# One transfer for each copy of x, and fp32 products in layer 0 of a recommender tower

## The chip, the cores and the metric

The kernel runs on one core of a Trainium2 chip. The metric is the device time of one execution in microseconds (us), the median of some runs. The core has five engines with instruction streams of their own, which meet only through semaphores: PE (TensorE, matrix products), DVE (VectorE), ACT (ScalarE), POOL (GpSimd) and SP, which issues most of the DMA transfers. Sixteen DMA engines carry the transfers of all queues.

## The reference

A compressed interaction network over looked-up embeddings, then a small dense tower. 1024 rows of the batch, 32 fields, 16 embedding columns, three layers of 128 outputs:

```python
e = jnp.stack([tbl_0[ids[:, 0]], ..., tbl_31[ids[:, 31]]], axis=1)     # 1024 x 32 x 16
x0 = h = e
for i in range(3):
    z = (x0[:, :, None, :] * h[:, None, :, :]).reshape(B, F * G, E)
    y = relu(einsum('oc,bce->boe', W[i], z) + b[i][None, :, None])
    x_keep, h = (y[:, :64], y[:, 64:]) if i < 2 else (y, y)
    xs.append(x_keep)
z = sum(concatenate(xs, axis=1), axis=2)                               # 1024 x 256
h = maximum(concatenate([z, dense_ctx], axis=1) @ W_top1 + b_top1, 0)
h = maximum(h @ W_top2 + b_top2, 0)
return h @ W_top3
```

Everything is float32. Layer 0 has 32 x 32 products of fields with themselves (symmetric, so that half of them suffice), layers 1 and 2 have 32 x 64 each.

## The kernel before

**Tiles.** A block is 128 rows of the batch, a tile is four embedding columns of a block: 512 columns (`COLS`) with 48 rows (`XROWS`, the 32 fields and the first 16 again). There are 32 tiles. On the partitions lie pairs of a field and a second index, 128 at a time; such a set is a chunk, two chunks are an item, and an item is one DVE product of 128 x 1024. Layer 0 has two items, (0, 0) and (0, 1), and a tail of one chunk, layers 1 and 2 have eight items each, (1, 0) to (2, 7).

**Copies of x.** To multiply x by itself shifted, and by h, x must lie on the partitions in several copies. ACT copies the transposed x into `xrows` (48 x 512), SP stores it in DRAM as `xcols` (line 383), waits until that has landed, and loads it back: `shifted` in four transfers, one for each group of 32 partitions (line 390), `shifted_tail` in four (line 395), and `spread` in groups of four chunks, two transfers for each group, one per half of 64 partitions, each of which repeats a row of x on 64 partitions (line 406). `spread` has two buffers, for even and odd tiles, and a group is loaded again once DVE has made the last product that reads it (the wait on `s_made` in `load_spread`).

**Order.** `SLOT` writes out the order of the items; all engines follow it. Slot s does layer 1 of tile s, layer 2 of tile s - 1 and layer 0 of tile s + 1, interleaved. SP does for each tile, in `load_factors`: `load_shifted` of the tile, the last group of `spread` for the tile before it, then groups 0 to 2 of its own. SP works strictly in that order, so a wait holds up all that stands behind it. The middle of the program is a hardware loop over blocks.

**Precision.** PE multiplies plain fp32 items (`WHOLE`, line 604), as layer 1 is done. The others are split: ACT rounds the product to fp32r (`high`, line 808), DVE or POOL subtracts to get the rest (`low`, lines 1051 and 490), and PE makes three passes with weights split the same way: high by high, high by low (line 612) and low by high (line 627). `kind_of` says which item is of which kind: layer 1 whole, layer 0 and item (2, 6) split by DVE, the rest of layer 2 by POOL; in the last slot other items of layer 2 go to DVE. Each kind has a ring of buffers, `RING = (4, 4, 2)`. POOL also does the lookups (line 480).

**Before the loop** the weights are transposed by PE and put in place by DVE, from a layout of layer 0 (`w0_dist`) in which chunk after chunk holds the field distances. `rotated` prepares the first tile's `shifted` without DRAM.

Of the kernel before, what the change touches and what calls it, by code (L numbers as in the profile page):

```python
# [33 lines left out]
F32 = mybir.dt.float32  # L34
# [4 lines left out]
P = 128  # L39
FIELDS = 32  # L40
# [44 lines left out]
RING = (4, 4, 2)  # L85
SPLIT2_BY_DVE = [(2, 6)]
LAST_BY_DVE = [(2, 2), (2, 5), (2, 7)]
# [74 lines left out]
def dlrm_tower(nc, dense_ctx, ids, tables, w_top1, b_top1, w_top2, b_top2, w_top3,  # L162
               w0, b0, w1, b1, w2, b2, xcols, out):
    batch = ids.shape[0]
# [6 lines left out]
    with ExitStack() as ctx:  # L171
# [21 lines left out]

        w0T_high = sb("w0T_high", [P, GROUP, P], F32R)
        w0T_low = sb("w0T_low", [P, GROUP, P], F32R)
# [3 lines left out]
        w2T_low = sb("w2T_low", [P, CHUNKS, P], F32R)  # L199
        wt3 = sb("wt3", [P, TOP2 // P])  # L200

# [165 lines left out]
        def _(sp):  # L367
# [11 lines left out]
            def load_shifted(t):  # L379


                sp.wait_ge(s_xrows, number(t) + 1)
                sp.dma_start(xcols[number(t)], xrows[:, :]).then_inc(s_xcols, 16)
                sp.wait_ge(s_xcols, 16 * (number(t) + 1))
                x = xcols[number(t)]
                if isinstance(t[0], int) and number(t) == 0:

                    return
                for j in range(GROUP):
                    sp.dma_start(shifted[FIELDS * j:FIELDS * (j + 1), :, :],  # L390
                                 bass.AP(x.tensor, x.offset + j * COLS,
                                         [[COLS, FIELDS], [GROUP * COLS, GROUP], [1, COLS]])
                                 ).then_inc(s_shifted, 16)
                for j in range(GROUP):
                    sp.dma_start(shifted_tail[FIELDS * j:FIELDS * (j + 1), :],
                                 x[FIELDS // 2:XROWS, :]).then_inc(s_shifted_tail, 16)

            def load_spread(t, g):
                x = xcols[number(t)]
# [42 lines left out]

            sp.wait_ge(s_made[BY_DVE], plan.entry((BLOCKS - 1, TILES_PER_BLOCK - 2), LAST0) + 1)
            sp.dma_start(wt1[:, :].rearrange("p (c n) -> p c n", n=TOP1),
# [95 lines left out]
        def _(pe):  # L540
# [8 lines left out]
            pe.wait_ge(s_ident, 1)  # L549
            pe.wait_ge(s_sym, 7)  # L550
            turn(0, GROUP, P, lambda c: w0_dist[:, P * c:P * (c + 1)])
# [17 lines left out]
            def turn_x(t):  # L569

                pe.wait_ge(s_four, number(t) + 1)
                if not (isinstance(t[0], int) and number(t) == 0):

                    pe.wait_ge(s_xrows, number(t))
                    pe.wait_ge(s_made[BY_DVE], plan.entry(after(t, -2), LAST0) + 1)
# [17 lines left out]
            def multiply(s, item):  # L593
# [6 lines left out]
                if kind == WHOLE:  # L600
                    z = prod[plan.place(s, item, RING)]
                    pe.wait_ge(s_made[kind], e + 1)
                    for c in range(ITEM):
                        last = pe.matmul(y[:, :], w1T[:, ITEM * n + c, :], z[:, c, :], start=(n == 0 and c == 0),  # L604
                                         stop=(item == LAST1 and c == ITEM - 1))
                    last.then_inc(s_used[kind], 1)
                else:
                    z = high[kind][plan.place(s, item, RING)]
                    pe.wait_ge(s_high[kind], e + 1)
                    for c in range(ITEM):  # L610
                        for w in ((w0T_high, w0T_low) if layer == 0 else (w2T_high, w2T_low)):
                            pe.matmul(y[:, :], w[:, ITEM * n + c, :], z[:, c, :],  # L612
                                      start=(n == 0 and c == 0 and w in (w0T_high, w2T_high)), stop=False)

            def multiply_low(s, item):
# [10 lines left out]
                for c in range(ITEM):  # L626
                    last = pe.matmul(accumulator(s, layer)[:, :], (w0T_high if layer == 0 else w2T_high)[:, ITEM * n + c, :],  # L627
                                     z[:, c, :], start=False, stop=(item in (LAST0, LAST2) and c == ITEM - 1))
                last.then_inc(s_used[kind], 1)
# [124 lines left out]
        def _(act):  # L754
# [29 lines left out]
            def take_x(t):  # L784
                act.wait_ge(s_xT, number(t) + 1)

                act.wait_ge(s_xcols, 16 * number(t))
                act.copy(xrows[:, :], xT[0:XROWS, :]).then_inc(s_xrows, 1)
# [21 lines left out]
            def next_h0(s):  # L810

                act.wait_ge(s_used[BY_DVE], plan.entry(s, LAST0) + 1)
                go_on(h0[(s[1] + 1) % 2], y0, 1, bias0, s_h0)
# [48 lines left out]
            def top_high(part):  # L862
# [10 lines left out]
                elif part == 3:  # L873
                    act.wait_ge(s_wt2, 16)

                    act.wait_ge(s_xT, TILES)
                    act.wait_ge(s_xcols, 16 * TILES)
                    copy = act.copy(wt2_high[:, :], wt2[:, :])
# [41 lines left out]
        def _(dve):  # L920
# [19 lines left out]
            dve.tensor_copy(w0_dist[:, FIELDS:FIELDS * H].rearrange("p (d f) -> p d f", f=FIELDS),  # L940
                            bass.AP(w0_wide.tensor, w0_wide.offset + 1,
                                    [list(w0_wide.ap[0]), [1, H - 1], [2 * FIELDS + 1, FIELDS]])).then_inc(s_sym, 1)
            dve.tensor_copy(w0_dist[:, 0:FIELDS], diagonal(w0_raw, FIELDS, 0, FIELDS)).then_inc(s_sym, 1)
# [4 lines left out]

            dve.wait_ge(s_sym, 6)
# [3 lines left out]
            homes = [w0T_high[:, :, :], w0T_tail[:, :]]  # L953
            homes += [w1T[:, GROUP * g:GROUP * (g + 1), :] for g in range(GROUPS)]
            homes += [w2T_high[:, GROUP * g:GROUP * (g + 1), :] for g in range(GROUPS)]
            lows = {0: w0T_low[:, :, :]}
            lows.update({2 + GROUPS + g: w2T_low[:, GROUP * g:GROUP * (g + 1), :] for g in range(GROUPS)})
            for n, home in enumerate(homes):
                dve.wait_ge(s_turned, n + 1)
                source = prep[1][:, 0, :] if n == 1 else prep[n % 2]  # L960
                if n == 1:
# [7 lines left out]
                    last.then_inc(s_stored, 1)  # L969
                elif n in lows:  # L970
                    dve.tensor_copy(home, source).then_inc(s_w_high, 1)

# [30 lines left out]
            for c in FIRST_ORDER:  # L1003
                dve.tensor_copy(rotated[c].rearrange("p (e a f) -> p e a f", a=GROUP, f=FIELDS),
                                bass.AP(unwrapped.tensor, unwrapped.offset + GROUP * c,
                                        [list(unwrapped.ap[0]), [XROWS, QUAD], [1 if c < GROUP else 0, GROUP], [1, FIELDS]])
                                ).then_inc(s_rotated, 1)

            def multiply(s, item):
# [6 lines left out]
                elif item == (0, 0):  # L1016
                    dve.wait_ge(s_shifted, 16 * GROUP * number(t))
                if item == (0, 0):
                    dve.wait_ge(s_xT, number(t) + 1)
                if item == TAIL:  # L1020
                    if not isinstance(t[0], int) or number(t) > 0:
                        dve.wait_ge(s_shifted_tail, 16 * GROUP * number(t))

# [177 lines left out]
```

## Time and profile before

| | us |
|---|---|
| median of 3 runs | 1115.0 |
| lowest and highest run | 1112.32 and 1119.09 |
| span of the profiled execution | 1109.1 |
| busy PE / DVE / POOL / ACT in it | 994.0 / 987.2 / 882.4 / 572.7 |

The span is the time from the first to the last instruction of the profiled execution; the runs also hold what lies around it. An engine's busy time leaves out its waits and its semaphore instructions. PE's busy time counts pipelined matmuls, whose ends are modelled, so starts that follow one another say more of its pace. Mean times in the groups come with a count, and "idle before" tells how long the engine stood just before such instructions and who released it.

### The profile page before, as it was taken

The numbers are of one execution on the slowest core, as the hardware profiler recorded it, in microseconds if no ns is written. First come the engines' busy times: TensorE is split into PE (matmuls) and PEld (weight loads), VectorE is DVE, ScalarE is ACT, GpSimd is POOL, SyncE is SP. The second block draws the span as 40 slices with busy tenths as digits, with TensorE's granted clock in tenths as the row PEclk, the third lists the DMA queues.
The fourth block names the chain that finished last, engine by engine and source line by source line (L and its number), as shares of the span: only waits on it lengthen the run. The fifth ranks groups of instructions, "written<-read, shape, count | busy, mean of one in ns | idle before, by whom it ended". The sixth has DMA issues, their size and how long they took to land.

```text
span 1109.1 us, 12343 instructions
## 1 busy us (share of the span) xinstructions
PE 994.0 (90%) x3281; PEld 611.0 (55%) x3281; DVE 987.2 (89%) x842; ACT 572.7 (52%) x683; POOL 882.4 (80%) x525
## 2 busy tenths in 40 slices
PE   3167989998997979999899989999899999999988
PEld 2134556564654646555556656555556656565665
DVE  6246999999996999999999999999999999999982
ACT  0234556554654545565555645565455556555553
POOL 7645899997977979997999979997999966665760
PEclk9588999998998999999899999999899999999999
DMA  6199989899886869898888879888788989888500
GB/s 118 14 195 198 184 170 190 195 186 191 168 192 133 164 163 199 175 194 177 168 183 182 195 174 193 184 186 190 156 182 179 192 194 191 185 197 193 124 1 1
DMA packets 111813, 184.55 MB, mean 166 GB/s; under 512 B 19570, under 2 KB 24178, under 8 KB 111540
## 3 DMA queue, kind: packets, MB, share of 16 engines
q1 hardware_dynamic: 103604, 182.24, 76.8%
q0 software_dynamic: 8192, 2.11, 1.9%
q8 instruction: 8, 0.13, 0.1%
q14 instruction: 9, 0.07, 0.0%
HBM read 181.15 MB, written 3.15 MB: 166 GB/s over the span
## 4 chain that ended last, share of the span: by engine, by line
POOL 29%; DVE 18%; issue 18%; DMA 15%; PE 13%; ACT 4%; SPq 2%; DVEq 1%; POOLq 0%; ACTq 0%
POOL low L490 15%; POOL looked_up L480 12%; DVE unsplit L1043 9%; DMA xcols<-xrows 6%; PE y L604 6%; DMA shifted<-xcols 5%; DVE prod L1043 4%; PE y L612 4%; PE y L627 2%; POOL tail_parts L498 2%; DMA spread<-xcols 1%; SPq L390 1%; DMA looked_up<-in_tbl,ids_now 1%; ACT h L794 1%; DVE tail L1025 1%
## 5 line engine op out<-in xcount | busy, mean ns | idle before, releaser
L490 POOL TENSOR_TENSOR low<-unsplit,high 128x1024 fp32r<-128x1024 f32 x222 | 543.7, 2454 | 110.5 <-ACT high L808 108.3
L808 ACT CAST high<-unsplit 128x1024 fp32r<-128x1024 f32 x320 | 334.0, 1047 | 330.2 <-DVE unsplit L1043 322.7
L604 PE MATMUL y<-prod,w1T 128*128 128x512 f32 x1024 | 491.4, 609 | 5.1 <-ACT kept L800 2.7
L480 POOL DMA_INDIRECT looked_up<-in_tbl,ids_now x256 | 291.3, 1138 | 69.3 <-issue 58.6
L1043 DVE TENSOR_TENSOR prod<-spread,h 128x1024 f32<-128x1024 f32 x256 | 307.1, 1210 | 7.9 <-ACT h L794 7.4
L1043 DVE TENSOR_TENSOR unsplit<-spread,h 128x1024 f32<-128x1024 f32 x256 | 307.7, 1212 | 4.2 <-ACT h L794 4.2
L604 PEld LDWEIGHTS y<-prod,w1T 128*128 128x128 f32 x1024 | 196.0, 195 | 171.1 <-issue 149.5
L627 PE MATMUL y<-low,w2T_high 128*128 128x512 f32 x512 | 222.5, 518 | 48.4 <-POOL low L490 47.5
L612 PE MATMUL y<-high,w2T_high 128*128 128x512 f32 x512 | 217.1, 424 | 5.7 <-ACT high L808 5.5
L1051 DVE TENSOR_TENSOR low<-unsplit,high 128x1024 fp32r<-128x1024 f32 x98 | 187.3, 1911 | 22.3 <-ACT high L808 22.3
L612 PE MATMUL y<-high,w2T_low 128*128 128x512 f32 x512 | 202.9, 396 | 0.0
L627 PEld LDWEIGHTS y<-low,w2T_high 128*128 128x128 f32 x512 | 93.8, 192 | 147.9 <-POOL low L490 83.3
L794 ACT ACTIVATE h<-y,bias 64x512 f32<-64x512 f32 x128 | 83.3, 651 | 69.7 <-PE y L604 44.5
L612 PEld LDWEIGHTS y<-high,w2T_high 128*128 128x128 f32 x512 | 96.6, 189 | 40.8 <-ACT high L808 15.4
L612 PEld LDWEIGHTS y<-high,w2T_low 128*128 128x128 f32 x512 | 96.5, 188 | 28.2 <-issue 7.4
L1043 DVE TENSOR_TENSOR unsplit<-shifted,xT 128x1024 f32<-128x1024 f32 x64 | 77.8, 1216 | 35.9 <-DMA shifted<-xcols 34.4
L612 PE MATMUL y<-high,w0T_high 128*128 128x512 f32 x128 | 53.1, 415 | 9.5 <-ACT high L808 9.5
L612 PE MATMUL y<-high,w0T_low 128*128 128x512 f32 x128 | 52.8, 412 | 0.0
L498 POOL TENSOR_TENSOR tail_parts<-tail,tail_high 128x512 fp32r<-128x512 f32 x32 | 41.3, 1290 | 12.9 <-ACT tail_high L832 12.9
L800 ACT ACTIVATE kept<-y,bias_kept 64x512 f32<-64x512 f32 x64 | 43.8, 685 | 1.6
L1074 DVE TENSOR_TENSOR acc_kept<-acc_kept,kept 128x512 f32<-128x512 f32 x24 | 44.2, 1843 | 0.0
L627 PE MATMUL y<-low,w0T_high 128*128 128x512 f32 x128 | 41.8, 410 | 0.0
(114 smaller groups left out, 482.4 us busy)
## 6 DMA issues: line engine op xcount, KB each, us to landing
spread<-xcols SPq DMA_DIRECT2D x256, 512.0 KB, 6.9
shifted<-xcols SPq DMA_DIRECT2D x124, 256.0 KB, 4.6
shifted_tail<-xcols SPq DMA_DIRECT2D x124, 64.0 KB, 4.9
looked_up<-in_tbl,ids_now POOLq DMA_INDIRECT x256
xcols<-xrows SPq DMA_DIRECT2D x32, 96.0 KB, 5.5
spread<-in_L_rec_W SPq DMA_DIRECT2D x3, 512.0 KB, 7.1
spread<-in_L_rec_W SPq DMA_DIRECT2D x1, 1024.0 KB, 10.9
wt<-in_W_top SPq DMA_DIRECT2D x2, 512.0 KB, 9.4
```

Source lines behind the costliest of these rows:

```text
L480: pool.indirect_dma_start(out=looked_up[:, f, :], out_offset=None, in_=tables[f][:, :], in_offset=bass.IndirectOffsetOnAxis(ap=ids_now[:, ...
L490: pool.tensor_tensor(low[kind][r][:, :, :], unsplit[kind][r][:, :, :], high[kind][r][:, :, :].bitcast(F32), ALU.subtract).then_inc(s_low[k ...
L498: pool.tensor_tensor(tail_parts[:, :], tail[:, :], tail_high[:, :].bitcast(F32), ALU.subtract).then_inc(s_tail_low, 1)
L604: last = pe.matmul(y[:, :], w1T[:, ITEM * n + c, :], z[:, c, :], start=(n == 0 and c == 0), stop=(item == LAST1 and c == ITEM - 1))
L612: pe.matmul(y[:, :], w[:, ITEM * n + c, :], z[:, c, :], start=(n == 0 and c == 0 and w in (w0T_high, w2T_high)), stop=False)
L627: last = pe.matmul(accumulator(s, layer)[:, :], (w0T_high if layer == 0 else w2T_high)[:, ITEM * n + c, :], z[:, c, :], start=False, stop= ...
L794: last = act.activation(h[to, :], y[lanes, :], ACT.Relu, bias=bias[lanes, :])
L800: act.activation(kept[t[1] % 2][lanes, :], y[lanes, :], ACT.Relu, bias=bias_kept[lanes, :]).then_inc(s_kept, 1)
L808: act.copy(high[kind][r][:, :, :], unsplit[kind][r][:, :, :]).then_inc(s_high[kind], 1)
L1043: dve.tensor_tensor(z, x[:, ITEM * n:ITEM * (n + 1), :], b[:, :].unsqueeze(1).to_broadcast([P, ITEM, COLS]), ALU.mult).then_inc(s_made[kin ...
L1051: dve.tensor_tensor(low[kind][r][:, :, :], unsplit[kind][r][:, :, :], high[kind][r][:, :, :].bitcast(F32), ALU.subtract).then_inc(s_low[ki ...
L1074: dve.tensor_tensor(acc_kept[:, :], acc_kept[:, :], z[:, :], ALU.add).then_inc(s_sum_kept, 1)
```

## The change

Both parts are in one edit. First, each copy of x is brought by one transfer to all 128 partitions. `shifted` takes four neighbouring rows of `xcols` at once for each partition (8 KB), which gives the chunks of layer 0 another order: the weights' layout `w0_dist` and `rotated` change with it. For `spread` a second array in DRAM is written for each tile, `xpairs`, with the even fields first and then the odd ones, so that four chunks' rows lie together (8 KB) for each half of the partitions. Counts that are waited for change with the number of transfers. Second, layer 0 and item (2, 6) of layer 2 are whole: no cast, no subtraction, plain fp32 products with unsplit weights, `w0T` and `w2T_whole`, in the ring of whole items.

```diff
-SPLIT2_BY_DVE = [(2, 6)]
+WHOLE2 = (2, 6)
...
-    if item[0] == 1:
+    if item[0] < 2 or item == WHOLE2:
         return WHOLE
-    return BY_DVE if item[0] == 0 or item in (LAST_BY_DVE if last else SPLIT2_BY_DVE) else BY_POOL
+    return BY_DVE if last and item in LAST_BY_DVE else BY_POOL
...
                 sp.dma_start(xcols[number(t)], xrows[:, :]).then_inc(s_xcols, 16)
-                sp.wait_ge(s_xcols, 16 * (number(t) + 1))
+                pairs = xpairs[number(t)]
+                sp.dma_start(bass.AP(pairs.tensor, pairs.offset,
+                                     [[COLS, FIELDS // 2], [FIELDS // 2 * COLS, 2], [1, COLS]]),
+                             xrows[0:FIELDS, :]).then_inc(s_xcols, 16)
+
+                sp.wait_ge(s_xcols, 32 * (number(t) + 1))
...
-                for j in range(GROUP):
-                    sp.dma_start(shifted[FIELDS * j:FIELDS * (j + 1), :, :],
-                                 bass.AP(x.tensor, x.offset + j * COLS,
-                                         [[COLS, FIELDS], [GROUP * COLS, GROUP], [1, COLS]])
-                                 ).then_inc(s_shifted, 16)
-                for j in range(GROUP):
-                    sp.dma_start(shifted_tail[FIELDS * j:FIELDS * (j + 1), :],
-                                 x[FIELDS // 2:XROWS, :]).then_inc(s_shifted_tail, 16)
+                sp.dma_start(shifted[:, :, :],
+                             bass.AP(x.tensor, x.offset,
+                                     [[GROUP * COLS, GROUP], [COLS, FIELDS], [1, GROUP * COLS]])
+                             ).then_inc(s_shifted, 16)
+                sp.dma_start(shifted_tail[:, :],
+                             bass.AP(x.tensor, x.offset + FIELDS // 2 * COLS,
+                                     [[0, GROUP], [COLS, FIELDS], [1, COLS]])).then_inc(s_shifted_tail, 16)
...
-                for half in range(2):
-                    sp.dma_start(spread[k % 2][HALF * half:HALF * (half + 1), GROUP * g:GROUP * (g + 1), :],
-                                 bass.AP(x.tensor, x.offset + (2 * GROUP * g + half) * COLS,
-                                         [[0, HALF], [2 * COLS, GROUP], [1, COLS]])
-                                 ).then_inc(s_spread[k % 2][g], 16)
+                sp.dma_start(spread[k % 2][:, GROUP * g:GROUP * (g + 1), :],
+                             bass.AP(x.tensor, x.offset + GROUP * g * COLS,
+                                     [[FIELDS // 2 * COLS, 2], [0, HALF], [1, GROUP * COLS]])
+                             ).then_inc(s_spread[k % 2][g], 16)
...
-                        last = pe.matmul(y[:, :], w1T[:, ITEM * n + c, :], z[:, c, :], start=(n == 0 and c == 0),
-                                         stop=(item == LAST1 and c == ITEM - 1))
+                        w = w2T_whole[:, c, :] if layer == 2 else (w0T, w1T)[layer][:, ITEM * n + c, :]
+                        last = pe.matmul(y[:, :], w, z[:, c, :], start=(n == 0 and c == 0),
+                                         stop=(item in (LAST0, LAST1) and c == ITEM - 1))
...
+            for a in range(GROUP):
+
+                dve.tensor_copy(w0_dist[:, P * a:P * (a + 1)].rearrange("p (j f) -> p j f", f=FIELDS),
+                                bass.AP(w0_wide.tensor, w0_wide.offset + a,
+                                        [list(w0_wide.ap[0]), [GROUP, GROUP], [2 * FIELDS + 1, FIELDS]])).then_inc(s_sym, 1)
...
-                        dve.wait_ge(s_spread[t[1] % 2][n // (GROUP // ITEM)], 32 * uses_of_parity(t))
+                        dve.wait_ge(s_spread[t[1] % 2][n // (GROUP // ITEM)], 16 * uses_of_parity(t))
```

## Rows read from the trace of the kernel before

**Rows 1.** The page: its header, busy time of the engines, the chain by engine.

```profile
span 1109.1 us, 12343 instructions
...
PE 994.0 (90%) x3281; PEld 611.0 (55%) x3281; DVE 987.2 (89%) x842; ACT 572.7 (52%) x683; POOL 882.4 (80%) x525
...
POOL 29%; DVE 18%; issue 18%; DMA 15%; PE 13%; ACT 4%; SPq 2%; DVEq 1%; POOLq 0%; ACTq 0%
```

**Rows 2.** Timeline of SP, several stretches: start us, us, queue, line, transfer, count.

```profile
51.44 0.35 SPq L383 DMA_DIRECT2D xcols<-xrows  x1
53.45 0.66 SPq L406 DMA_DIRECT2D spread<-xcols  x1
...
158.73 0.36 SPq L383 DMA_DIRECT2D xcols<-xrows  x1
...
631.99 0.36 SPq L383 DMA_DIRECT2D xcols<-xrows  x1
638.39 1.47 SPq L390 DMA_DIRECT2D shifted<-xcols  x3
...
999.83 0.43 SPq L383 DMA_DIRECT2D xcols<-xrows  x1
```

**Rows 3.** Timeline of PE's weight loads from 602.9 us: split passes, then plain.

```profile
602.93 0.19 PEld L612 LDWEIGHTS y<-high,w2T_high 128*128 128x128 f32 x1
603.16 0.19 PEld L612 LDWEIGHTS y<-high,w2T_low 128*128 128x128 f32 x1
...
604.53 0.19 PEld L604 LDWEIGHTS y<-prod,w1T 128*128 128x128 f32 x1 [0.24 <-issue]
604.96 0.19 PEld L604 LDWEIGHTS y<-prod,w1T 128*128 128x128 f32 x1 [0.24 <-issue]
```

**Rows 4.** DMA, whole span: SP's queue, then issues (KB each, us to landing).

```profile
q1 hardware_dynamic: 103604, 182.24, 76.8%
...
spread<-xcols SPq DMA_DIRECT2D x256, 512.0 KB, 6.9
shifted<-xcols SPq DMA_DIRECT2D x124, 256.0 KB, 4.6
shifted_tail<-xcols SPq DMA_DIRECT2D x124, 64.0 KB, 4.9
...
xcols<-xrows SPq DMA_DIRECT2D x32, 96.0 KB, 5.5
```

**Rows 5.** Busy time in 612 to 631 us, then clock, DMA share, GB/s.

```profile
core 0: us, PE busy (x) PEld busy (x) DVE busy (x) ACT busy (x) POOL busy (x), PEclk, DMA share, GB/s
612.00:631.00 19.00, 19.00 (x67) 12.10 (x66) 18.84 (x19) 10.56 (x13) 17.53 (x12) 1.00 0.91 197
```

**Rows 6.** Waits, the engines' and SP's: us in total, times, longest us.

```profile
ACT emb L772 <- DMA looked_up<-in_tbl,ids_now: 45.8, 8, 18.1
...
DVE unsplit L1043 <- DMA shifted<-xcols: 34.4, 18, 7.0
...
SPq L406 <- DVE unsplit L1043: 424.3, 62, 10.9
SPq L390 <- DMA xcols<-xrows: 151.3, 31, 7.2
```

**Rows 7.** DMA in 3 to 4 us, then in 3.8 to 4.6 us.

```profile
DMA packets 52, 0.21 MB, mean 213 GB/s; under 512 B 0, under 2 KB 0, under 8 KB 52
...
q1 hardware_dynamic: 52, 0.21, 76.0%
...
DMA packets 81, 0.33 MB, mean 415 GB/s; under 512 B 8, under 2 KB 8, under 8 KB 73
...
q1 hardware_dynamic: 81, 0.33, 104.8%
```

**Rows 8.** Timeline of DVE from 1059 us: the first product of the last slot.

```profile
1059.70 2.35 DVE L1043 TENSOR_TENSOR unsplit<-spread,h 128x1024 f32<-128x1024 f32 x2 [1.32 <-ACT h L794]
```

**Rows 9.** Groups by line: busy us, mean ns, then idle before and releaser.

```profile
L490 POOL TENSOR_TENSOR low<-unsplit,high 128x1024 fp32r<-128x1024 f32 x222 | 543.7, 2454 | 110.5 <-ACT high L808 108.3
L808 ACT CAST high<-unsplit 128x1024 fp32r<-128x1024 f32 x320 | 334.0, 1047 | 330.2 <-DVE unsplit L1043 322.7
...
L1051 DVE TENSOR_TENSOR low<-unsplit,high 128x1024 fp32r<-128x1024 f32 x98 | 187.3, 1911 | 22.3 <-ACT high L808 22.3
```

More of the change, by code:

```diff
@@ L162, in dlrm_tower @@
 def dlrm_tower(nc, dense_ctx, ids, tables, w_top1, b_top1, w_top2, b_top2, w_top3,
-               w0, b0, w1, b1, w2, b2, xcols, out):
+               w0, b0, w1, b1, w2, b2, xcols, xpairs, out):
     batch = ids.shape[0]
@@ L199, in dlrm_tower @@
         w2T_low = sb("w2T_low", [P, CHUNKS, P], F32R)
+        w2T_whole = sb("w2T_whole", [P, ITEM, P])
         wt3 = sb("wt3", [P, TOP2 // P])
@@ L388, in load_shifted @@
                     return
-                for j in range(GROUP):
-                    sp.dma_start(shifted[FIELDS * j:FIELDS * (j + 1), :, :],
-                                 bass.AP(x.tensor, x.offset + j * COLS,
-                                         [[COLS, FIELDS], [GROUP * COLS, GROUP], [1, COLS]])
-                                 ).then_inc(s_shifted, 16)
-                for j in range(GROUP):
-                    sp.dma_start(shifted_tail[FIELDS * j:FIELDS * (j + 1), :],
-                                 x[FIELDS // 2:XROWS, :]).then_inc(s_shifted_tail, 16)
+                sp.dma_start(shifted[:, :, :],
[5 more added lines that the diff above has]
+                                     [[0, GROUP], [COLS, FIELDS], [1, COLS]])).then_inc(s_shifted_tail, 16)
             def load_spread(t, g):
-                x = xcols[number(t)]
+                x = xpairs[number(t)]
                 k = t[1]
@@ L549, in _ @@
             pe.wait_ge(s_ident, 1)
-            pe.wait_ge(s_sym, 7)
+            pe.wait_ge(s_sym, 10)
             turn(0, GROUP, P, lambda c: w0_dist[:, P * c:P * (c + 1)])
@@ L574, in turn_x @@
                     pe.wait_ge(s_xrows, number(t))
-                    pe.wait_ge(s_made[BY_DVE], plan.entry(after(t, -2), LAST0) + 1)
+                    pe.wait_ge(s_made[WHOLE], plan.entry(after(t, -2), LAST0) + 1)
                 for e in range(QUAD):
@@ L610, in multiply @@
                     for c in range(ITEM):
-                        for w in ((w0T_high, w0T_low) if layer == 0 else (w2T_high, w2T_low)):
+                        for w in (w2T_high, w2T_low):
                             pe.matmul(y[:, :], w[:, ITEM * n + c, :], z[:, c, :],
-                                      start=(n == 0 and c == 0 and w in (w0T_high, w2T_high)), stop=False)
+                                      start=(n == 0 and c == 0 and w is w2T_high), stop=False)
             def multiply_low(s, item):
@@ L626, in multiply_low @@
                 for c in range(ITEM):
-                    last = pe.matmul(accumulator(s, layer)[:, :], (w0T_high if layer == 0 else w2T_high)[:, ITEM * n + c, :],
-                                     z[:, c, :], start=False, stop=(item in (LAST0, LAST2) and c == ITEM - 1))
+                    last = pe.matmul(accumulator(s, layer)[:, :], w2T_high[:, ITEM * n + c, :],
+                                     z[:, c, :], start=False, stop=(item == LAST2 and c == ITEM - 1))
                 last.then_inc(s_used[kind], 1)
@@ L785, in take_x @@
                 act.wait_ge(s_xT, number(t) + 1)
-                act.wait_ge(s_xcols, 16 * number(t))
+                act.wait_ge(s_xcols, 32 * number(t))
                 act.copy(xrows[:, :], xT[0:XROWS, :]).then_inc(s_xrows, 1)
@@ L876, in top_high @@
                     act.wait_ge(s_xT, TILES)
-                    act.wait_ge(s_xcols, 16 * TILES)
+                    act.wait_ge(s_xcols, 32 * TILES)
                     copy = act.copy(wt2_high[:, :], wt2[:, :])
@@ L947, in _ @@
                             diagonal(w0_raw, FIELDS, H * FIELDS, H)).then_inc(s_sym, 1)
-            dve.wait_ge(s_sym, 6)
+            dve.wait_ge(s_sym, 9)
             once = w0_dist[:, FIELDS * H:FIELDS * (H + 1)]
@@ L952, in _ @@
                             once.unsqueeze(1).to_broadcast([P, GROUP - 1, FIELDS])).then_inc(s_sym, 1)
-            homes = [w0T_high[:, :, :], w0T_tail[:, :]]
+            homes = [w0T[:, :, :], w0T_tail[:, :]]
             homes += [w1T[:, GROUP * g:GROUP * (g + 1), :] for g in range(GROUPS)]
             homes += [w2T_high[:, GROUP * g:GROUP * (g + 1), :] for g in range(GROUPS)]
-            lows = {0: w0T_low[:, :, :]}
-            lows.update({2 + GROUPS + g: w2T_low[:, GROUP * g:GROUP * (g + 1), :] for g in range(GROUPS)})
+            lows = {2 + GROUPS + g: w2T_low[:, GROUP * g:GROUP * (g + 1), :] for g in range(GROUPS)}
             for n, home in enumerate(homes):
@@ L970, in _ @@
                 elif n in lows:
+                    if WHOLE2[1] // (GROUP // ITEM) == n - 2 - GROUPS:
+                        of = ITEM * WHOLE2[1] % GROUP
+                        dve.tensor_copy(w2T_whole[:, :, :], source[:, of:of + ITEM, :])
                     dve.tensor_copy(home, source).then_inc(s_w_high, 1)
@@ L1016, in multiply @@
                 elif item == (0, 0):
-                    dve.wait_ge(s_shifted, 16 * GROUP * number(t))
+                    dve.wait_ge(s_shifted, 16 * number(t))
                 if item == (0, 0):
@@ L1194 @@
     xcols = nc.dram_tensor("xcols", (tiles, XROWS, COLS), F32, kind="Internal").ap()
+    xpairs = nc.dram_tensor("xpairs", (tiles, FIELDS, COLS), F32, kind="Internal").ap()
     out = nc.dram_tensor("out", (batch, 1), F32, kind="ExternalOutput").ap()
@@ L1197 @@
                dram("W_top2"), dram("b_top2"), dram("W_top3"), dram("L0_rec_W0"), dram("L0_rec_b0"),
-               dram("L0_rec_W1"), dram("L0_rec_b1"), dram("L0_rec_W2"), dram("L0_rec_b2"), xcols, out)
+               dram("L0_rec_W1"), dram("L0_rec_b1"), dram("L0_rec_W2"), dram("L0_rec_b2"), xcols, xpairs, out)
     result = run_bass_kernel_spmd(nc, [arrays], core_ids=[0])
```

17 lines of the change are left out of this document (7 added, 10 removed).

## Prediction

> **What bounds the kernel now.** I read the page's header, busy shares and chain first. PE is busy 90% of the span and DVE 89%, POOL 80%, and no engine holds the chain: POOL 29%, DVE and pure issue 18% each, DMA 15%, PE 13% [rows 1]. Such a mixture means a pipeline in which several engines are close to full. The reader should see next how long one tile takes. The stores of x that SP issues (line 383) come once a tile: 158.73 us and 999.83 us are 28 tiles apart, so a tile takes 841.10 / 28 = 30.04 us [rows 2]. Then PE's own need: weight loads of the split passes follow one another by 0.23 us (602.93, 603.16), those of the plain fp32 products by 0.43 us (604.53, 604.96) [rows 3]. One chunk of 128 product rows costs three split passes, 0.69 us, or one plain product, recorded as two matmuls, 0.86 us. A tile has 16 plain chunks (layer 1) and 20 split chunks (4 of layer 0, 16 of layer 2): 13.8 + 13.8 us, and some 0.8 us of tail and transposes, 28.4 us in all. PE has 1.6 us to spare in each tile.
>
> The transfers are the other resource near its limit. The SP queue holds 76.8% of the 16 DMA engines for the whole span and moved 182.24 MB [rows 4]: 182,240 / (0.768 x 16 x 1109.1) = 13.4 KB/us, that is 13.4 B/ns, for each busy DMA engine. In the middle of a tile the share is 0.91 at 197 GB/s [rows 5], again 13.5 B/ns. Of these bytes 256 x 512 KB are the copies of x in `spread` [rows 4]: 4 MiB in each tile, for one tile in every 30 us. So the kernel needs about 14 of its 16 DMA engines. DVE lost 34.4 us waiting for `shifted`, SP 151.3 us waiting for the store of x to land, and SP 424.3 us for buffers of `spread` [rows 6]; this last wait is only slack.
>
> **The change, DMA part.** A tile's 16 issues (8 for spread, 4 shifted, 4 tail) become 6, and the store gets a twin, `xpairs`, 64 KB. Bytes into the chip's buffers stay the same, and rows become 8 KB where they were 2 KB. Issue time falls: eight loads of `spread` at 0.6 us become four, and nothing waited for SP's issue for long. That is worth nothing by itself.
>
> What decides is how a transfer is dealt out to the 16 engines. The transfers of before all have an outermost dimension of 32, 48, 64 or 128 rows on both sides, and their rows show all 16 engines at work. The new source patterns begin otherwise: `[2][64 copies][2048]` for spread, `[4][32][2048]` for shifted, `[4 copies][32][512]` for the tail. The destination is 128 partitions. If a copy is cut along the outermost dimension of its patterns, the new spread load can be cut in 2 at most, the others in 4. Each half of spread is then one engine's work. I assume further that a transfer on fewer engines always begins with the same one, so that the same two engines get every load of spread and their queue carries everything. [...]
> [...]
>
> The price goes by how fast one engine is. Bounds: in the first microseconds the weights arrive in 8 KB rows. From 3 to 4 us, 213 GB/s at a share of 76.0% is 213 / 16 / 0.760 = 17.5 B/ns; from 3.8 to 4.6 us, 415 GB/s at 104.8% is 24.7 B/ns, and 25.9 if the overlap of packets is not divided out [rows 7]. All these have 16 engines competing; with two alone I take 25 B/ns, near the faster row. For the whole:
> - spread: 1 MiB over 2 engines is 524,288 B each, 524,288 / 25 = 21.0 us; 4 x 32 = 128 of them, 2684 us.
> - shifted: 1 MiB over 4 is 262,144 B, 10.5 us; tail: 256 KiB over 4, 2.6 us; by the same assumption both lie on the two loaded engines and two more. Stores of x: 160 KB over 16 engines, 0.8 us. Together 13.9 us in each of 31 tiles.
> - a gap in each tile: SP waits for the store to land before it issues shifted, and behind that wait stand the tail and the last group of `spread`. The store itself queues on the two loaded engines behind the groups already issued, so their queue is empty when it lands. With idle DMA engines this took 2.01 us (51.44 to 53.45), in the busy middle 6.4 us (631.99 to 638.39) [rows 2]. I take 4 us.
> - 31 x (13.9 + 4) = 555 us.
> - before the first load of spread: 53.45 us [rows 2] and 2.5 us for the second store and the start.
> - after the last group lands: five products of that slot, about 6 us, then the last slot and the top layers, which run now from 1059.70 to the end at 1109.1, 49 us [rows 8]: 55 us.
> Sum: 56 + 2684 + 555 + 55 = 3350 us of span. The median of the runs, 1115.0, is 5.9 us above the profiled span; with this 3355 us. A tile takes about 4 x 21.0 + 17.9 = 102 us. The other loads of a tile can't fill the gap: groups 0 to 2 of the next tile stand on SP behind the last group of this one.
> [...]
> Bounds of this case, from the rows: at 25.9 B/ns and a 2 us gap, 2591 + 31 x (13.4 + 2) + 111 + 6 = 3185 us; at 17.5 B/ns and 6.4 us, 3835 + 31 x (19.5 + 6.4) + 111 + 6 = 4755 us. At 13.5 B/ns, the present rate of 2 KB rows, it would be some 6060; the rows are 8 KB and 14 engines fewer compete, so I don't reach for it.
>
> **The change, fp32 part.** Layer 0 and item (2, 6) become plain: 4 x 32 + 2 x 31 = 190 chunks go from 0.69 to 0.86 us on PE [rows 3], plus 1.0 us a tile, 32 us. DVE loses 95 of its 98 subtractions at 1911 ns, 181 us, ACT 95 casts at 1047 ns, 99 us [rows 9]. POOL keeps its own 222 subtractions; at 2454 ns they may become shorter as DVE's, which read two SBUF operands beside them, go. The ring of whole items is then used by 11 items a tile where it was 8, with 4 buffers as before: DVE waits there for PE somewhat earlier. In the preparation three more copies for the weights of layer 0 and one for `w2T_whole` cost 0 to 1.5 us under the weights' own loads. In the case above all this lies beside transfers of 102 us a tile and costs nothing; if the transfers stay wide, it decides.
>
> **Rivals.** Each supposes that all 16 engines share the new transfers, say because the division goes by the 128 partitions.
> - Slower by PE. For: PE is 90% busy and gets 1.0 us more a tile, and the spare 1.6 us are waits of the pipeline (ACT's 45.8 us for `looked_up` in 8 blocks [rows 6]), which DVE's relief doesn't touch. Then 30.04 + 1.0 a tile: 1115 + 32 = 1147 us.
> - Not slower, here faster. The 5.5 MB of a tile at 17.5 instead of 13.5 B/ns per engine take 20 us of 16 engines where they took 25, so `shifted` arrives in time; the cover that DVE and POOL lacked is there. It decides once the waits of a tile shrink by more than PE's 1.0 us. At most all 1.6 us go: 29.4 us a tile, 1115 - 32 x 0.64 = 1095 us. Against: the waits for looked_up stay, and only part of the chain was DMA [rows 1].
> - Between these two it is within 0.5%, 1109 to 1121 us. That the change would then not do what it says (fewer, longer transfers with no gain) is this case.
>
> **How the numbers follow.** Narrow transfers: 0.83. All engines share and slower: 0.05; and faster: 0.08; and unchanged within 0.5%, about what a measurement of this kernel can tell: 0.04. Predicted time 3355 us. The range is that of the narrow case, from 3100 (a little under its lower bound, since two engines alone may beat any row here) to 4800; what it leaves out is 0.17 of the wide cases and about 0.03 of its own. Faster 0.08, same 0.04, slower 0.88.
>
> **What would show it.** [...] SP's wait for the store grows to 60 us and more, as it queues. The rate: packets of 8 KB at 8192 / 25 = 328 ns each. The fp32 part: 95 subtractions fewer at line 1051's successor. Wrong: a DMA share above 0.6 would drop the narrow case at once, and then a tile's period against 31.0 and 29.4 us tells the two rivals apart. A time of 2900 would mean that one engine is faster than every row of before; 4700, that it stays at 17.5 B/ns even alone.

## The result, and the profile after

The changed kernel takes 3334.7 us (median of 4 runs, 3327.95 to 3343.32) beside 1117.05 us for the kernel before on the same chip: 2.983 times as long, 95% interval 2.972 to 2.994. The forecast was 3355 us. The profiled execution spans 3330.9 us.

The page of the changed kernel: busy time of the engines, the busy tenths of DMA in 40 slices, SP's queue, the chain by engine and by line.

```profile
span 3330.9 us, 11034 instructions
...
PE 1303.4 (39%) x3089; PEld 685.8 (21%) x3089; DVE 779.8 (23%) x750; ACT 471.8 (14%) x587; POOL 816.7 (25%) x524
...
DMA  3111111111111111111111111111111111111110
...
q1 hardware_dynamic: 36524, 184.30, 15.2%
...
DMA 61%; SPq 31%; issue 2%; DVE 2%; POOL 1%; PE 1%; another core or an unknown queue 1%; ACT 0%; DVEq 0%; ACTq 0%; POOLq 0%
DMA spread<-xpairs 35%; DMA xpairs<-xrows 24%; SPq L383 18%; SPq L409 12%; DMA wt<-in_W_top 1%; DVE unsplit L1053 1%; POOL looked_up L483 1%; SPq L398 1%; SPq L394 1%; DVE prod L1053 0%; DVE low L1061 0%; PE y L608 0%; DVEq L1050 0%; PE y L712 0%
```

Against [rows 1] and [rows 4]: the same 182 to 184 MB now hold 15.2% of the 16 DMA engines over a span three times as long, where they held 76.8%. No engine is busy half of the time, and DMA and SP, which feeds it, are 92% of the chain. By line the loads of `spread` are 35% of it, the landing of the store of `xpairs` 24%, and the issue of the store of x (L383) 18%. The page shows no clearer sign of a transfer that runs on few engines than this pair: a chain of DMA with a DMA share near 2 of 16.

One tile on SP, timeline:

```profile
1530.66 0.63 SPq L394 DMA_DIRECT2D shifted<-xcols  x1
1531.49 0.55 SPq L398 DMA_DIRECT2D shifted_tail<-xcols  x1
1532.33 53.69 SPq L409 DMA_DIRECT2D spread<-xpairs  x4
1586.42 19.18 SPq L383 DMA_DIRECT2D xcols<-xrows  x1
1605.78 2.01 SPq L385 DMA_DIRECT2D xpairs<-xrows  x1
1630.70 0.61 SPq L394 DMA_DIRECT2D shifted<-xcols  x1
```

And the two stretches of it that hold one kind of transfer each, from the DMA view; first 1560 to 1580 us (spread alone), then 1533 to 1543 us (shifted, with the first spread group behind it):

```profile
q1 hardware_dynamic: 130, 1.05, 12.6%
...
q1 hardware_dynamic: 85, 0.70, 25.7%
```

A tile takes 100.0 us here. While spread loads, 12.6% of 16 engines is 2.0 engines, and they move 1.05 MB in 20 us: 1050 / (0.126 x 16 x 20) = 26.0 B/ns each. While shifted loads, 25.7% is 4.1 engines, at 700 / (0.257 x 16 x 10) = 17.0 B/ns; from 1543 to 1548 us it is 86 GB/s at a share of 0.25, 21.5 B/ns. The source of spread begins with 2 and that of shifted with 4, so both numbers are those of the engines at work.

Who waits, the views of waits of the engines and of SP:

```profile
DVE prod L1053 <- DMA spread<-xpairs: 1371.3, 95, 17.6
DVE prod L1053 <- DMA shifted<-xcols: 1064.1, 31, 37.0
...
SPq L394 <- DMA xpairs<-xrows: 712.0, 31, 23.5
```

DVE, which waited 34.4 us for shifted before [rows 6], waits 2435 us for the two copies of x, and that is more than the whole increase of the span, 2222 us. Not all of the 1064 us for shifted is its own transfer. In the tile shown DVE stood from 1514.4 us, and SP could ask for shifted only at 1530.66, when the store of `xpairs`, issued at 1507.30 behind the loads of spread, had landed. About half of that wait is the store's.

### The profile page after: what moved, and what is told of

It is laid out like the page before. It is cut to its first block, busy times and chain, and to the rows that moved or that the text cites. A ratio compares the mean times of both kernels' runs of the same rounds, so it can differ in the third digit from the quotient of the medians.

```text
span 3330.9 us, 11034 instructions
## 1 busy us (share of the span) xinstructions
PE 1303.4 (39%) x3089; PEld 685.8 (21%) x3089; DVE 779.8 (23%) x750; ACT 471.8 (14%) x587; POOL 816.7 (25%) x524
## 3 DMA queue, kind: packets, MB, share of 16 engines
q1 hardware_dynamic: 36524, 184.30, 15.2%
## 4 chain that ended last, share of the span: by engine, by line
DMA 61%; SPq 31%; issue 2%; DVE 2%; POOL 1%; PE 1%; another core or an unknown queue 1%; ACT 0%; DVEq 0%; ACTq 0%; POOLq 0%
DMA spread<-xpairs 35%; DMA xpairs<-xrows 24%; SPq L383 18%; SPq L409 12%; DMA wt<-in_W_top 1%; DVE unsplit L1053 1%; POOL looked_up L483 1%; SPq L398 1%; SPq L394 1%; DVE prod L1053 0%; DVE low L1061 0%; PE y L608 0%; DVEq L1050 0%; PE y L712 0%
## 5 line engine op out<-in xcount | busy, mean ns | idle before, releaser
L608 PE MATMUL y<-prod,w1T 128*128 128x512 f32 x1024 | 673.1, 800 | 1006.5 <-DVE prod L1053 1006.5
L1053 DVE TENSOR_TENSOR prod<-spread,h 128x1024 f32<-128x1024 f32 x288 | 344.9, 1216 | 1418.0 <-DMA spread<-xpairs 1371.3
L812 ACT CAST high<-unsplit 128x1024 fp32r<-128x1024 f32 x224 | 234.3, 1046 | 2601.3 <-DVE unsplit L1053 2601.2
L608 PE MATMUL y<-prod,w0T 128*128 128x512 f32 x256 | 179.0, 838 | 960.3 <-DVE prod L1053 960.3
L608 PEld LDWEIGHTS y<-prod,w1T 128*128 128x128 f32 x1024 | 248.8, 254 | 1277.1 <-DVE prod L1053 1002.4
L1053 DVE TENSOR_TENSOR prod<-shifted,xT 128x1024 f32<-128x1024 f32 x64 | 77.8, 1218 | 1067.4 <-DMA shifted<-xcols 1064.1
L608 PEld LDWEIGHTS y<-prod,w0T 128*128 128x128 f32 x256 | 62.0, 257 | 1032.8 <-DVE prod L1053 886.0
L483 POOL DMA_INDIRECT looked_up<-in_tbl,ids_now x256 | 247.3, 966 | 66.5 <-issue 52.0
L616 PE MATMUL y<-high,w2T_high 128*128 128x512 f32 x448 | 253.8, 566 | 14.6 <-ACT high L812 14.6
L798 ACT ACTIVATE h<-y,bias 64x512 f32<-64x512 f32 x128 | 83.3, 651 | 71.6 <-PE y L608 70.1
L608 PE MATMUL y<-prod,w2T_whole 128*128 128x512 f32 x128 | 60.1, 592 | 0.0
```

The lines of the kernel that those rows point to most:

```text
L483: pool.indirect_dma_start(out=looked_up[:, f, :], out_offset=None, in_=tables[f][:, :], in_offset=bass.IndirectOffsetOnAxis(ap=ids_now[:, ...
L608: last = pe.matmul(y[:, :], w, z[:, c, :], start=(n == 0 and c == 0), stop=(item in (LAST0, LAST1) and c == ITEM - 1))
L616: pe.matmul(y[:, :], w[:, ITEM * n + c, :], z[:, c, :], start=(n == 0 and c == 0 and w is w2T_high), stop=False)
L798: last = act.activation(h[to, :], y[lanes, :], ACT.Relu, bias=bias[lanes, :])
L812: act.copy(high[kind][r][:, :, :], unsplit[kind][r][:, :, :]).then_inc(s_high[kind], 1)
L1053: dve.tensor_tensor(z, x[:, ITEM * n:ITEM * (n + 1), :], b[:, :].unsqueeze(1).to_broadcast([P, ITEM, COLS]), ALU.mult).then_inc(s_made[kin ...
```

## The experiments

The theory: each transfer is cut along the outermost dimension of its patterns, and the part thus left idle explains the time. The rivals: the fp32 part has a share in it; the 8 KB rows, the second store or the repeated source are slow in themselves; a single transfer to 128 partitions is.

### Each part alone

The kernel before with the DMA part of the change and nothing of the fp32 part (`SPLIT2_BY_DVE`, `w0T_high`, `w0T_low` and the split products stay):

```diff
                 sp.dma_start(xcols[number(t)], xrows[:, :]).then_inc(s_xcols, 16)
-                sp.wait_ge(s_xcols, 16 * (number(t) + 1))
+                pairs = xpairs[number(t)]
+                sp.dma_start(bass.AP(pairs.tensor, pairs.offset,
+                                     [[COLS, FIELDS // 2], [FIELDS // 2 * COLS, 2], [1, COLS]]),
+                             xrows[0:FIELDS, :]).then_inc(s_xcols, 16)
+
+                sp.wait_ge(s_xcols, 32 * (number(t) + 1))
...
+                sp.dma_start(spread[k % 2][:, GROUP * g:GROUP * (g + 1), :],
+                             bass.AP(x.tensor, x.offset + GROUP * g * COLS,
+                                     [[FIELDS // 2 * COLS, 2], [0, HALF], [1, GROUP * COLS]])
+                             ).then_inc(s_spread[k % 2][g], 16)
```

> The DMA part alone: new transfers, products split as before. Theory (each transfer is cut along the outermost dimension of its patterns, so spread runs on 2 engines and shifted and tail on 4): the products hide beside transfers of 100 us a tile, so 3320 to 3350 us, as with both parts. Rival (the fp32 part takes a share of the loss, by starving the ring of whole items): clearly less, under 3200 us.

Measured: 3331.0 us in one run, span 3329.1, against 3334.7 with both parts. The whole loss is the DMA part's.

The fp32 part alone is the other half of the diff, with the transfers of before:

```diff
-    if item[0] == 1:
+    if item[0] < 2 or item == WHOLE2:
         return WHOLE
```

> The fp32 part alone: transfers as before. PE gets 190 chunks at 0.17 us more, 32 us, DVE loses 95 subtractions, 181 us. If PE's need is what counts: 1117 + 32 = 1149 us. If the waits of a tile shrink by more than PE's 1.0 us: down to 1095 us. I take the first to be a little likelier, 1130.

Measured: 1105.3 us, ratio 0.988 (0.985 to 0.991). The estimate of 1130 was wrong in its sign. Timeline of SP, the fifth and the last of the 32 stores of x, as in [rows 2]; then a wait and two groups of the page:

```profile
160.08 0.35 SPq L383 DMA_DIRECT2D xcols<-xrows  x1
...
993.56 0.34 SPq L383 DMA_DIRECT2D xcols<-xrows  x1
```

```profile
PEld y L628 <- POOL low L490: 50.6, 79, 7.1
...
L490 POOL TENSOR_TENSOR low<-unsplit,high 128x1024 fp32r<-128x1024 f32 x221 | 530.1, 2405 | 151.6 <-ACT high L809 149.1
...
L480 POOL DMA_INDIRECT looked_up<-in_tbl,ids_now x256 | 249.7, 975 | 75.0 <-issue 66.4
```

The lines of the kernel before that answer to the first and the last of these:

```profile
PEld y L627 <- POOL low L490: 83.3, 78, 7.4
...
L480 POOL DMA_INDIRECT looked_up<-in_tbl,ids_now x256 | 291.3, 1138 | 69.3 <-issue 58.6
```

The fifth and the last store are 27 tiles apart, so a tile takes 833.48 / 27 = 30.87 us here, and 841.10 / 27 = 31.15 us in the kernel before. The prediction divided by 28 and had 30.04 us, which is too short. By its estimate PE's need rose from 28.4 to 29.4 us a tile, so PE's spare time fell from 2.7 to 1.5 us: the waits shrank by a little more than the need grew. Of the 27 intervals between these stores 21 were shorter than 31 us before, with a mean of 29.69 us, and 22 are now, with 29.73; in these PE is now within about 0.3 us of its estimated need. The gain lies in the long intervals, 217.7 us in six of them before and 179.3 us in five now.

What shrank are, among others, waits for POOL: PE's weight loads waited 83.3 us for its subtractions before and 50.6 now, POOL's subtractions take 2405 ns instead of 2454 [rows 9], and issuing a lookup takes 975 ns instead of 1138. The lookups get shorter with the fp32 part whatever the transfers are: 1144 ns in wide_rows_split and 972 in both_parts_wide, 1064 in dma_part_alone and 966 in the changed kernel. DVE's subtractions and ACT's casts both go with that part, and neither was tried apart, so which of them shortens the lookups isn't shown.

### The same rows and bytes on all 16 engines

Both parts, but in the pieces of before, with 64 and 32 partitions and the same 8 KB rows:

```diff
-                sp.dma_start(spread[k % 2][:, GROUP * g:GROUP * (g + 1), :],
-                             bass.AP(x.tensor, x.offset + GROUP * g * COLS,
-                                     [[FIELDS // 2 * COLS, 2], [0, HALF], [1, GROUP * COLS]])
-                             ).then_inc(s_spread[k % 2][g], 16)
+                for half in range(2):
+                    sp.dma_start(spread[k % 2][HALF * half:HALF * (half + 1), GROUP * g:GROUP * (g + 1), :],
+                                 bass.AP(x.tensor, x.offset + (FIELDS // 2 * half + GROUP * g) * COLS,
+                                         [[0, HALF], [1, GROUP * COLS]])
+                                 ).then_inc(s_spread[k % 2][g], 16)
```

> Both parts, but the transfers issued in pieces as before: two halves of 64 partitions for each spread group, four of 32 for shifted and for the tail. The rows stay 8 KB and the bytes, the layouts and xpairs are those of the changed kernel; only the outermost dimensions are again 64 and 32. Theory: all 16 engines work, 1095 to 1149 us. Rival (8 KB rows read over and over, or the second store, are slow in themselves): over 2000 us.

Measured: 1106.6 us, ratio 0.990 (0.988 to 0.993). Layouts, bytes, row length, the second store and the order are those of the changed kernel; giving up the single transfer takes away 2228 us.

The same pieces without the fp32 part:

> 8 KB rows in pieces on 16 engines as in both_parts_wide, products split as before: what long rows alone are worth. DMA engines at 17.5 instead of 13.5 B/ns leave more of them idle, and the 34.4 us that DVE waited for shifted shrink; the second store costs some 0.5 us in each tile's wait for the store. 1100 to 1117 us; the rival, that transfers were hidden anyway, gives 1117 and more.

Measured: 1119.5 us, ratio 1.001 (0.9995 to 1.003). Long rows, taken together with the second store that they need, are worth nothing: DVE's wait for shifted shrank from 34.4 to 24.6 us, and no shorter time follows from it. The kernel before was not bound by these loads.

### Which of the transfers

Only spread as single transfers, then only shifted and the tail, the others in pieces of 64 and 32 partitions as above.

> Of the changed kernel only spread stays in single transfers (outermost dimension 2), shifted and tail go in four pieces. With packets of 313 ns for 8 KB, 26.2 B/ns, 128 transfers take 2561 us on 2 engines; shifted on 16 engines adds some 5 us a tile, tail 1, stores 1, the gap 2: 31 x 9 = 279 us; ends 110 us. 2950 us. Were shifted and tail the larger part of the loss, it would be under 2000.

Measured: 2921.9 us. The step is right within 1%: spread accounts for most of the loss.

> Only shifted and tail stay single transfers (outermost dimension 4), spread goes in halves of 64 partitions. The four loaded engines have 262 + 66 KB for shifted and tail and 262 KB of spread for each tile, 590 KB; at 16 to 17 B/ns about 36 us and 2 us of gap, so 38 us a tile and 1280 us in all; at 13.5 B/ns 1450 us. A rival in which the four engines are not the same as those of spread's shares (any four, in turn) would hide it: 1106 us.

Measured: 1610.4 us, above what I expected. The two stores of x shown are 48.1 us apart, and the waits say why:

```profile
588.21 0.34 SPq L383 DMA_DIRECT2D xcols<-xrows  x1
...
636.35 0.34 SPq L383 DMA_DIRECT2D xcols<-xrows  x1
...
DVE prod L1054 <- DMA shifted<-xcols: 595.0, 31, 30.5
```

I had added up the bytes of the four loaded engines as if they could be busy all the time. But `shifted` is asked for only once its x exists and is needed by the middle of the same slot, so DVE stood 595.0 / 31 = 19.2 us in each tile, and these add to the 29 us of the products. In the tile shown shifted is issued at 592.77 us and DVE goes on at 620.38. This slow transfer on the path cost its latency, 19.2 us a tile, not its share of an engine. This also means that the run doesn't test the rival of other engines in turn: shifted would be late on any four.

### The number at the outside of the source

To give a single spread transfer another outermost dimension, `xpairs` holds each half of x several times. Shifted and tail stay in pieces. For 4 (and so for 8 and 16):

```diff
-                sp.dma_start(bass.AP(pairs.tensor, pairs.offset,
-                                     [[COLS, FIELDS // 2], [FIELDS // 2 * COLS, 2], [1, COLS]]),
-                             xrows[0:FIELDS, :]).then_inc(s_xcols, 16)
+                for copy in range(2):
+                    sp.dma_start(bass.AP(pairs.tensor, pairs.offset + copy * FIELDS // 2 * COLS,
+                                         [[COLS, FIELDS // 2], [2 * FIELDS // 2 * COLS, 2], [1, COLS]]),
+                                 xrows[0:FIELDS, :]).then_inc(s_xcols, 16)
...
-                                     [[FIELDS // 2 * COLS, 2], [0, HALF], [1, GROUP * COLS]])
+                                     [[FIELDS // 2 * COLS, 4], [0, P // 4], [1, GROUP * COLS]])
```

> As spread_narrow, but xpairs holds each half twice (one more store of 64 KB a tile), and the single spread transfer reads [4][32][2048]: outermost dimension 4. Theory: 4 engines. At 26.2 B/ns 10.0 us for each transfer, 40 + 9 us a tile, 1680 us; at 16.4 B/ns, the pace of the four engines that carry shifted in the changed kernel, 64 + 9, 2370 us. Rival (a repeated source is what makes it slow, not the outermost count): still 2950 us.

> xpairs holds each half four times, single spread transfers with outermost dimension 8. Theory: 8 engines, 512 KB a tile on each: 20 us at 26.2 B/ns, hidden in part under the 30 us of the products, 1110 to 1200 us; 38 us at 13.5 B/ns, plus 9, 1550 us. Rival: still 2950 us.

> xpairs holds each half eight times (eight stores of 64 KB a tile), single spread transfers read [16][8][2048]: outermost dimension 16. Theory: 16 engines, the loss of the changed kernel is gone though each copy is still one transfer to 128 partitions: 1105 to 1150 us, above both_parts_wide by what the seven further stores delay shifted. Rival (a single transfer to 128 partitions with a repeated source is slow in itself): over 1500 us.

Measured: 1836.5, 1579.8 and 1118.2 us (one run each for the first two, 8 for the last, ratio 1.005, 1.003 to 1.007). SP's queue, from the DMA view: copies4 in 610 to 620 us, copies8 in 527 to 537 us, both while spread loads and little else does, and copies16 in 300 to 1000 us:

```profile
q1 hardware_dynamic: 168, 1.10, 27.3%
...
q1 hardware_dynamic: 169, 1.16, 50.5%
...
q1 hardware_dynamic: 31408, 136.68, 87.7%
```

27.3% is 4.4 engines (0.25 to 0.27, 4.0 to 4.3 engines, once the stores at the start of this stretch have passed) and 50.5% is 8.1. With spread single throughout, the time is 2922, 1836, 1580 and 1118 us for 2, 4, 8 and 16. A repeated source and 128 partitions are common to all four, so neither makes the transfer slow. The number of different rows that are read isn't what sets the number of engines either: each half in both_parts_wide reads one row 64 times and keeps 84.2% of 16 engines busy, and shifted in the changed kernel, which reads 44 different stretches of 8 KB, runs on 4.1. All numbers tried are powers of two, so the runs don't show what a number that doesn't divide evenly would do. The step from 4 to 8 gains little, for each busy engine then moves 1160 / (0.505 x 16 x 10) = 14.4 B/ns, where 4 engines moved 1100 / (0.273 x 16 x 10) = 25.2 B/ns. That copies16 loses against both_parts_wide is most likely because eight stores of `xpairs` stand between x and shifted: DVE waits 69.7 us for shifted where it waited 15.5. It waits longer for spread too, 17.9 us where it was 2.2.

### What the pace of an engine depends on

The blocks of `xpairs` farther apart in copies8 (`BLOCK_ROWS` is 19 where it was 16):

```diff
-                                     [[FIELDS // 2 * COLS, 8], [0, P // 8], [1, GROUP * COLS]])
+                                     [[BLOCK_ROWS * COLS, 8], [0, P // 8], [1, GROUP * COLS]])
```

> As copies8, but the eight blocks of xpairs lie 38 KB apart instead of 32 KB. In copies8 a packet of 8 KB took 577 ns, with 2 engines 315 ns. If the eight engines collide in DRAM because their rows lie a power of two apart: near 315 to 400 ns, and some 1200 us. If they collide at the partitions they write, or the pace is that of eight engines whatever they read: 577 ns and 1580 us again.

Measured: 1582.2 us, the same as copies8. Moving the blocks from 32 to 38 KB apart changes nothing, so their distance of a power of two is not the cause.

Spread loaded with rows of the weights of layer 2, 128 different rows of 8 KB, in halves and then whole; layers 1 and 2 of the tower are computed from these in place of x:

```diff
-                                 bass.AP(x.tensor, x.offset + (FIELDS // 2 * half + GROUP * g) * COLS,
-                                         [[0, HALF], [1, GROUP * COLS]])
+                                 w2[HALF * half:HALF * (half + 1), :]
```

```diff
-                             bass.AP(x.tensor, x.offset + GROUP * g * COLS,
-                                     [[FIELDS // 2 * COLS, 2], [0, HALF], [1, GROUP * COLS]])
+                             w2[:, :]
```

> As both_parts_wide, but the two transfers of each group read 64 different rows of the weights of layer 2 in place of one row of x repeated 64 times: the products of layers 1 and 2 are then of other data, the work is the same. Packets took 594 ns in both_parts_wide. If reading one row with all engines at once is what slows them: near 315 to 400 ns. If it is that all 16 engines write into the same half of the partitions: 594 ns again. The time stays 1100 to 1110 us either way, since PE sets it.

> As spread_narrow, but each single transfer to 128 partitions reads the 128 rows of the weights of layer 2, outermost dimension 128 on both sides (products of other data, same work). Theory: 16 engines, 1100 to 1115 us in place of 2922: what made the single transfer slow was the 2 at the outside of its source, not its 128 partitions or its size. Rival: still over 2000 us. Packets, if the partitions' half is what limits: 315 to 400 ns, otherwise 594 ns.

Measured: 1103.0 and 1083.4 us, one run each. SP's queue in 300 to 1000 us: both_parts_wide, then distinct rows in halves, then whole:

```profile
q1 hardware_dynamic: 25751, 128.94, 84.2%
...
q1 hardware_dynamic: 25827, 128.47, 84.4%
...
q1 hardware_dynamic: 24762, 131.14, 59.2%
```

The whole transfer is one DMA to all 128 partitions and it is fast: outermost dimension 128, and a share of 97.1% in 526 to 530 us, so 16 engines. That ends the rival that the single transfer itself is bad. Per busy engine the three move 13.7, 13.6 and 19.8 B/ns. Reading one row 64 times costs nothing against reading 64 rows. Halves of the partitions cost a third of the pace against the whole, by one run each. But copies16 also writes all 128 partitions in one transfer, and it moves only 136,680 / (0.877 x 16 x 700) = 13.9 B/ns. What sets the pace there wasn't tried.

## Why the prediction was right, point by point

- **What bounds the kernel before.** PE and POOL, with DMA near its limit but hidden. Right: wide_rows_split left the time where it was. The sum for a tile was wrong: 158.73 and 999.83 us are 27 tiles apart, not 28, so a tile took 31.15 us and PE had some 2.7 us to spare, not 1.6. The forecast of 3355 us doesn't use this figure. The reading that 14 of 16 engines are needed was too strong: distinct_rows_whole, one run on other data, moves as much with a share of 59.2%, so a high share need not be a need.
- **The cut along the outermost dimension.** No transfer in the rows of before has a small outermost dimension, so this was an estimate. It was right: a single transfer whose source begins with 2 ran on 2.0 engines (12.6%), with 4 on 4.1 (shifted, 25.7%) and 4.4 (copies4, 27.3%), with 8 on 8.1 (50.5%); with 16 the share is 87.7%, with 128 up to 97.1%. The small side was the source's each time and the other side 128 partitions; a small number on the destination's side wasn't tried. That the next load of spread gets the same two engines follows from the trace: SP had issued a second load of spread by 1546.89 us, the first landed at 1570.37, and from 1550 to 1570 us the share is still 12.6%. On two other engines the second would have run beside the first, at twice that share. And from 1533 to 1543 us, with shifted and the first load of spread both issued, the share is 25.7%, 4.1 engines and not 6, so the two of spread are among the four. Which two of the sixteen they are no view here shows.
- **One spread load 21.0 us at 25 B/ns.** Right: 20.2 us at 26.0 B/ns. The upper of the two rows of [rows 7], not divided by its overlap, was the closer one (25.9); no run shows why. 128 loads: 2581 us for 2684.
- **Shifted, tail and stores 13.9 us, the gap 4 us.** The first was too low, the second too high: here a term of the sum was mis-sized. DVE gets shifted at 1548.15, 17.5 us after its issue; the four engines ran at 17.0 to 21.5 B/ns, not 25. (The 0.8 us for the stores is a slip as well, 160 KB over 16 engines at 25 B/ns would be 0.4.) The DMA view shows the gap; slices of 1 us, from 1500 to 1540 us:

```profile
GB/s 49 49 66 49 49 49 57 129 121 49 49 66 49 49 49 49 66 49 54 52 65 58 50 49 49 49 66 49 45 29 4 0 49 74 66 66 49 82 57 74
```

  The queue runs dry at 1530 and moves again at 1532: 2 us, as with the idle engines of [rows 2]. The two slices of 129 and 121 are the store and lookups passing. Together, 20.2 us a tile for the 17.9 of the sum, some 70 us in all, where the spread term was 103 us too high. That the total came within 1% is in part luck: the two errors have opposite signs.
- **A tile 102 us.** The issues of shifted at 118.26 and 3145.39 us are 30 tiles apart, 100.9 us each.
- **Head 56 us and end 55 us.** The first load of spread goes out at 54.99 us. The end was 62 us and not 55: DVE's last wait for spread ends at 3268.58, and ACT waited 17.7 us, until 3269.92, for the weights of the top layers, which were issued at 3221.96 behind the last loads of spread; that this makes up the rest is an estimate.
- **The fp32 part costs nothing here.** Right: 3331.0 without it. The rivals for wide transfers turn on it, and there the one on the "not slower" side would have been right: 1106.6 us, ratio 0.990, between 1115 and its bound of 1095. I had given it 0.08 and the slower one 0.05. The argument for the slower one failed at the step that the spare time of a tile is made of waits that DVE's relief doesn't touch: of 2.7 us, 1.3 went in fp32_part_alone, more than PE's 1.0. The marks of 31.0 and 29.4 us for a tile's period would have misled, since they start from 30.04; both_parts_wide has 30.7 and is the faster kernel.
- **What would show it.** The DMA share came out at 0.16 and 57 GB/s. SP's wait for the store was to grow to 60 us: it is 23 us in the wait (712.0 / 31). With the issue itself, which I hadn't foreseen to take any time, it is 44 us from the store to shifted in the tile shown and 56 us in the one before it (1474.55 to 1530.66). The load of spread issued at 1532.33 us landed 38 us later. PE is busy 39% and DVE 23%. A recorded half of a plain product on PE takes 800 ns on average where it took 609, at a granted clock of 0.69 in 1000 to 3000 us, and DVE has the subtractions of the fp32 part less, 181 us by the prediction's count.

## What to carry to other kernels

Read the outermost dimension of a transfer's patterns before anything else. Here joined transfers whose source began with 2, 4 or 8 ran on 2.0, 4.4 and 8.1 of 16 engines and took 2922, 1836 and 1580 us; with 16 it was 1118 us, and with 128, on other data, 1083 us. A DMA share near so many sixteenths (12.6%, 27.3%, 50.5%) was its signature, with DMA in the chain (61% in the changed kernel). And a part that is neutral or good by itself (here the fp32 products, 1.2%) is invisible beside one that loses a factor, so time the parts apart: the fp32 part alone, at 1105.3 us, is as good as the best full version run here.

## What the runs showed of the hardware that I had not expected

- Issuing a transfer itself blocked. In the changed kernel the store of x at line 383 holds SP for 19.18 us, elsewhere 32.56 us, with no wait before it; before, the same instruction took 0.36 us [rows 2]. The longest is 33.15 us in spread_narrow, 3.46 in copies4 and 0.36 in copies8 and shifted_narrow, so it is long where spread is on two engines, and short or absent where it is on four or more. The cause isn't shown: no run looked at the queue itself.
- An engine's pace differs much with how many are at work and with the pattern: 26.0 B/ns with two, 25.2 with four (copies4) but 17.0 to 21.5 with the four of shifted, 14.4 with eight, 13.7 with sixteen in halves, and with sixteen over all partitions 19.8 in distinct_rows_whole but 13.9 in copies16. Why eight are as slow as sixteen stays open.
- distinct_rows_whole, at 1083.4 us, is 20 us faster than its twin in halves, though PE was taken to set both. DVE's wait for shifted falls from 16.2 to 7.6 us, PE's weight loads wait 38.3 us for POOL where they waited 53.3. It is a single run of a kernel that reads other data; what x itself would give with a source of 128 rows stays open; with 16 at the outside it is copies16.
- PE's granted clock is lower in this kernel, where PE is idle most of the time: 0.69 in 1000 to 3000 us, where it was 1.00 in [rows 5]. Two stretches of it (us, then busy time of PE, PEld, DVE, ACT, POOL, then the clock as a share, the DMA share and GB/s):

```profile
1560.00:1580.00 20.00, 11.20 (x31) 6.35 (x30) 5.75 (x5) 4.08 (x7) 10.07 (x7) 0.74 0.14 54
1533.00:1543.00 10.00, 0.00 (x0) 0.00 (x0) 0.00 (x0) 0.00 (x0) 0.00 (x0) 0.50 0.26 70
```

  In the second stretch PE does nothing, and the clock is at 0.50. From 1548 to 1552 us PE works again and the clock is still 0.50, from 1556 to 1560 it is 1.00. A recorded half of a plain product takes 800 ns on average where it took 609. I see no cost of this in the time, since DVE waits for the next load either way (1371.3 and 1064.1 us), but no run tried it apart.
